# Mixture-of-experts phase: GpSimd's gathers and scatters written out with indices taken from the table, expert numbers read once per tile, 71 blocks in place of 72

## The reference, cut to what matters

```python
logits = jnp.einsum('th,eh->te', x, gate_w)            # 8 experts
probs = jax.nn.softmax(logits.astype(jnp.float32), axis=-1)
topk_w, topk_i = jax.lax.top_k(probs, K)               # K = 2
...
g = jnp.einsum('th,ehi->eti', x, w_gate)               # 256 -> 352
u = jnp.einsum('th,ehi->eti', x, w_up)
eo = jnp.einsum('eti,eih->eth', jax.nn.silu(g) * u, w_down)
out = jnp.einsum('te,eth->th', combine, eo)
so = jax.nn.silu(x @ sw_gate) * (x @ sw_up) @ sw_down  # the shared expert
out = out + sg * so
```

## Time and profile before

| | us |
|---|---|
| median of 3 runs (2241.15 to 2248.3) | 2243.68 |
| the profiled execution, device time | 2245.09 |
| its span in the trace | 2243.4 |
| TensorE busy | 2090.2 (93%) |
| VectorE busy | 1318.9 (59%) |
| ScalarE busy | 1020.1 (45%) |
| GpSimd busy | 449.9 (20%) |

### The profile page before, as it was taken

How to read it: one execution, slowest core, us unless ns; L and a number is a source line. 1 busy time by engine, 2 the same in 40 slices (tenths; PEclk the granted TensorE clock), 3 DMA queues, 4 the chain that set the end, 5 groups by cost and what they waited for, 6 DMA issues and landing times. The chain is left out here.

```text
span 2243.4 us, 51733 instructions
## 1 busy us (share of the span) xinstructions
PE 2090.2 (93%) x18596; PEld 1403.1 (63%) x18597; DVE 1318.9 (59%) x2444; ACT 1020.1 (45%) x2049; POOL 449.9 (20%) x643
## 2 busy tenths in 40 slices
PE   6899799999999958999999999999988999999997
PEld 6577676766666734345556555555548676666665
DVE  5455448222222866789999999999725662222237
ACT  2211122222222123378989898898974222222221
POOL 1022100444444044400000000000000014444420
PEclk9999769999999979999999999999997899999999
DMA  7000010111111329601111111110032001111125
GB/s 282 0 1 0 22 54 3 54 56 56 57 58 54 122 70 218 160 22 45 46 49 40 47 46 46 43 45 20 3 151 93 11 19 57 56 57 58 58 80 178
DMA packets 92766, 142.37 MB, mean 63 GB/s; under 512 B 28724, under 2 KB 65844, under 8 KB 91380
## 3 DMA queue, kind: packets, MB, share of 16 engines
q1 hardware_dynamic: 77620, 98.02, 14.5%
q0 software_dynamic: 14976, 41.96, 5.7%
HBM read 91.04 MB, written 48.50 MB: 62 GB/s over the span
## 5 line engine op out<-in xcount | busy, mean ns | idle before, releaser
L1663 ACT ACTIVATE att_scores_pt<-att_scores_psE 128x512 f32<-128x512 f32 x1024 | 598.4, 598 | 68.4 <-PE att_scores_psE L1273 26.6
L1288 DVE TENSOR_REDUCE att_mx<-att_scores_psS 128x1 f32<-128x1024 f32 x472 | 578.1, 1225 | 50.0 <-PE att_scores_psS L1273 18.9
L592 PE MATMUL moe_ps<-W_gate_up,work 128*128 (+1 forms) x1664 | 535.3, 465 | 2.4 <-ACT work L269 1.2
L1273 PE MATMUL att_scores_psE<-att_qs,att_ks 99*32 99x512 bf16 x4096 | 436.7, 382 | 5.1 <-DVE att_scores_psO L1693 4.3
L592 PEld LDWEIGHTS moe_ps<-W_gate_up,work 128*128 128x128 f32 x1664 | 302.2, 192 | 143.5 <-issue 10.0
L615 PE MATMUL moe_ps<-W_down,moe_hidT 128*128 (+1 forms) x1248 | 318.6, 391 | 15.5 <-DVE moe_hidT L459 4.2
L1765 PE MATMUL att_scores_psO<-att_scores_pt,att_va 128*17 128x256 f32 x4096 | 330.0, 379 | 2.9 <-ACT att_scores_osb L1668 1.3
L1273 PE MATMUL att_scores_psS<-att_ks,att_qs 96*32 96x512 bf16 x3776 | 308.1, 380 | 0.1
L454 DVE TENSOR_TENSOR moe_hid<-moe_silu,moe_ps 128x352 f32<-128x352 f32 x208 | 108.3, 521 | 312.0 <-PE moe_ps L592 312.0
L615 PEld LDWEIGHTS moe_ps<-W_down,moe_hidT 128*128 128x128 f32 x1248 | 221.5, 190 | 65.3 <-issue 36.0
L273 ACT ACTIVATE moe_silu<-moe_ps 128x352 f32<-128x352 f32 x208 | 96.6, 464 | 337.9 <-PE moe_ps L592 337.9
(11 more groups left out here) (266 smaller groups left out, 2030.2 us busy)
## 6 DMA issues: line engine op xcount, KB each, us to landing
work<-expert_rows SPq DMA_DIRECT2D x64, 256.0 KB, 2.8
W_gate_up<-in_gate_up_dram SPq DMA_DIRECT2D x2, 6336.0 KB, 22.0
query_key_parts<-att_qkv_parts SPq DMA_DIRECT2D x32, 384.0 KB, 3.9
att_qs<-query_key_parts SPq DMA_DIRECT2D x96, 128.0 KB, 2.7
att_ks<-query_key_parts SPq DMA_DIRECT2D x96, 128.0 KB, 2.6
normalised_rows<-work SPq DMA_DIRECT2D x64, 128.0 KB, 1.7
W_down<-in_down_a_dram SPq DMA_DIRECT2D x2, 2304.0 KB, 27.0
values<-att_qkv_vt SPq DMA_DIRECT2D x32, 136.0 KB, 4.0
```

What stands on the lines that cost most here:

```text
L592: last = nc.tensor.matmul(bank[u][:, 0:I], srcT[u][:, k, :], W["gate_up"][:, k, e, half * I:(half + 1) * I], start=(k == 0), stop=(k == KD ...
L1273: last = nc.tensor.matmul(out[j:j + 32, :], stationary[:, j:j + 32], moving, start=True, stop=True, tile_position=(0, j), skip_group_check ...
L1288: return nc.vector.tensor_reduce(a.mx[g % 2][:, v:v + 1], bank[:, :, :].rearrange("p h k -> p (h k)"), AX.X, ALU.max)
L1663: nc.scalar.activation(pt[s % 2][:, r, :], psE[use % E_BANKS][:, :], ACT.Exp, scale=HD ** -0.5).then_inc(p_ready, 1)
```

## The change

- GpSimd: `fetch` no longer copies indices and no longer drains. Gather and scatter take their indices from `slots_i[:, j, 0:1]` and `slots_i[:, j, 1:2]`. Since j must be a plain number for that, the loop is gone and all blocks are written out.
- TensorE: `step` hands the expert's number on in a register. `next_e` is read behind `rows_in` of the tile ahead, and `before_e` is the register of the tile just done. At a loop's first tile nothing is handed on.
- `NB` is 71; the table keeps its 72 columns (`NBT`). The counts that buffers 0 to 5 wait for at the end are now `sent_by(u)`: 12 blocks for buffers 0 to 4 and 11 for buffer 5. VectorE peels 7 tiles in place of 6. TensorE's loop has the same 11 rounds, with two routed tiles behind it in place of three.

```diff
-            def fetch(j, u, free=None):
-
-                if free is not None:
-                    pool.wait_ge(y_sent[u], free)
+            def fetch(j):
+
+                u = j % SRC
+                if j >= SRC:
+                    pool.wait_ge(y_sent[u], j // SRC * 16)
                     pool.sem_inc(due, 1)
-                nc.gpsimd.tensor_copy(now_i[u][:, :], slots_i[:, j, :])
-                pool.drain()
                 nc.gpsimd.indirect_dma_start(
                     out=src[u][:, :], out_offset=None, in_=xn_d,
-                    in_offset=bass.IndirectOffsetOnAxis(ap=now_i[u][:, 0:1].bitcast(U32), axis=0)
+                    in_offset=bass.IndirectOffsetOnAxis(ap=slots_i[:, j, 0:1].bitcast(U32), axis=0)
                 ).then_inc(src_loaded[u], 16)
...
-            with pool.Fori(1, NB // SRC - 1) as jj:
-                for u in range(SRC):
-                    fetch(jj * SRC + (u + AHEAD), (u + AHEAD) % SRC, jj * 16 + (16 if u + AHEAD >= SRC else 0))
-                    send(jj * SRC + u, u)
-            for j in range(NB - SRC, NB):
+                fetch(j)
+            for j in range(NB):
                 if j + AHEAD < NB:
-                    fetch(j + AHEAD, (j + AHEAD) % SRC, (j + AHEAD) // SRC * 16)
-                send(j, j % SRC)
+                    fetch(j + AHEAD)
+                send(j)
...
+                here_e, before_e = known if known is not None else (expert(n, k), None)
                 if here:
                     hidden_T(n - 1, (here - 1) % 2)
-                gate_up(n, here % 2, expert(n, k))
+                gate_up(n, here % 2, here_e)
...
+                next_e = expert(n + 1, kind(here + 1)) if more else None
+                if here and before_e is None:
+                    before_e = expert(n - 1, kind(here - 1))
                 if here:
-                    down(n - 1, (here - 1) % 2, expert(n - 1, kind(here - 1)), kind(here - 2) if here >= 2 else None)
+                    down(n - 1, (here - 1) % 2, before_e, kind(here - 2) if here >= 2 else None)
+                return next_e, here_e
```

More of the change, by code:

```diff
@@ L21 @@
 KI = IP // P
-NB = (TOKENS * TOPK) // P + E
-SLOTS_ALL = NB * P
+NBT = (TOKENS * TOPK) // P + E
+NB = NBT - 1
+SLOTS_ALL = NBT * P
 ROWS_ALL = TOPK * TOKENS
@@ L102, in ffn_phase @@
         posf = sb("posf", [P, CH])
-        iota_p = sb("iota_p", [P, P], BF16); iota_j = sb("iota_j", [P, NB], BF16)
+        iota_p = sb("iota_p", [P, P], BF16); iota_j = sb("iota_j", [P, NBT], BF16)
         tile1 = sb("tile1", [P, CH], BF16)
         lane = sb("lane", [P, 1])
-        dump = sb("dump", [P, NB])
+        dump = sb("dump", [P, NBT])
         hot_p = [sb(f"hot_p{u}", [P, PIECE, P], BF16) for u in range(2)]
[L108 to L115, removed]
+        hot_j = sb("hot_j", [P, PIECE, NBT], BF16)
+        hot_id = [sb(f"hot_id{u}", [P, PIECE, 2, NBT], BF16) for u in range(2)]
+        place = sb("place", [P, NBT]); empty = sb("empty", [P, NBT])
+        slots_i = sb("slots_i", [P, NBT, 2], I32)
+        ble = sb("ble", [1, NBT, E])
+        bex = sb("bex", [1, NBT])
+        bexi = sb("bexi", [1, NBT], I32)
         ps = [ctx.enter_context(nc.psum_tensor(f"{tag}_ps{i}", [P, 512], F32)) for i in range(8)]
@@ L159, in ffn_phase @@
         buffer = lambda n0, u, k: (n0 - NA + u) % SRC if k == "routed" else (n0 + u) % 2
+        sent_by = lambda u: 16 * len(range(u, NB, SRC))
+        ROUNDS = NB // SRC
+        PEELED = 6 + NB % 2
         FOUND = 4 + CH // PIECE + 1
@@ L176, in _ @@
             for u in range(SRC):
-                sp.wait_ge(y_sent[u], 16 * (NB // SRC))
+                sp.wait_ge(y_sent[u], sent_by(u))
             for t in range(GS):
@@ L190, in _ @@
                            allow_small_or_imprecise_dtypes=True)
-            nc.gpsimd.iota(iotab[:, :], [[1, NB]], base=0, channel_multiplier=0,
+            nc.gpsimd.iota(iotab[:, :], [[1, NBT]], base=0, channel_multiplier=0,
                            allow_small_or_imprecise_dtypes=True)
@@ L221, in send @@
                 nc.gpsimd.indirect_dma_start(
-                    out=ys, out_offset=bass.IndirectOffsetOnAxis(ap=now_i[u][:, 1:2].bitcast(U32), axis=0),
-                    in_=yb[u % 2][:, :], in_offset=None).then_inc(y_sent[u], 16)
+                    out=ys, out_offset=bass.IndirectOffsetOnAxis(ap=slots_i[:, j, 1:2].bitcast(U32), axis=0),
+                    in_=yb[j % 2][:, :], in_offset=None).then_inc(y_sent[j % SRC], 16)
             pool.wait_ge(slots_ready, 1)
@@ L468, in source @@
                 if sent:
-                    dve.wait_ge(y_sent[u], 16 * (NB // SRC))
+                    dve.wait_ge(y_sent[u], sent_by(u))
                 else:
@@ L512, in _ @@
                 step(n, n, 0, "shared", finding.get(n, (lambda: one_hots(n - 4)) if 0 <= n - 4 < CH // PIECE else None))
-            with dve.Fori(0, (NB - 6) // 2) as i:
+            with dve.Fori(0, (NB - PEELED) // 2) as i:
                 for u in range(2):
                     step(i * 2 + (NA + u), NA, u, "routed")
-            for n in range(LAST - 6, LAST):
+            for n in range(LAST - PEELED, LAST):
                 step(n, n, 0, "routed")
@@ L649, in _ @@
                     with pe.Fori(0, times) as i:
+                        known = None
                         for u in range(UNROLL[k]):
-                            step(i * UNROLL[k] + (n0 + u), n0, u, k, i)
-                else:
-                    step(n0, n0, 0, k)
+                            known = step(i * UNROLL[k] + (n0 + u), n0, u, k, i, known, u + 1 < UNROLL[k])
+                    known = None
+                else:
+                    known = step(n0, n0, 0, k, 0, known, n0 + 1 < NS and n0 + 1 not in looped and n0 + 1 != NA)
+                    known = known if known[0] is not None else None
             hidden_T(NS - 1, (NS - 1) % 2)
```

30 lines of the change are left out of this document (14 added, 16 removed).

## The result

The changed kernel takes 2186.06 us (median of 4 runs, 2183.86 to 2187.8); the kernel before, run beside it, takes 2245.39. The ratio is 0.9733, with a 95% interval of 0.9718 to 0.9748: 2.7% faster. The profiled executions are 2245.09 us before and 2185.97 after, 59.1 us apart. The forecast was 46.2 us less on the same footing and 2198 us in all, with a range of 2188 to 2210.

The account below looks back on a forecast made before the run. GpSimd's 4.58 us round was taken to bound the routed tiles; 45.6 us from the routed stretches and 0.6 from the entries made 46.2 us saved, giving 2198 us, range 2188 to 2210.

Parts of the forecast that it names:

- What bounds the kernel: Routed tiles: GpSimd's round of drain, copy, issue and gather sets the pace, 4.58 us a block.
- Copy and drain gone, gap 0.30 us: GpSimd's routed blocks: gather follows scatter by 0.30 us instead of 2.10, making the round 2.58 us.
- Rival A: GpSimd: the 2.10 us gap belongs to the gather, so its round is 4.38 us and the kernel 2203; chance 0.12.
- B: GpSimd: a fresh index column costs 2.10 us, so scatters pay too, 6.18 us a block, about 2455 us; chance 0.03.
- The expert number handed on, 4.29 to 4.21 us: TensorE's routed tile: one read fewer ahead of gate and up shortens it from 4.29 to 4.21 us.
- The round's edge: TensorE's loop round of six tiles: 0.31 us as today plus 0.20 for a third read, 25.77 us in all.
- Rival D: TensorE's loop: the round's extra 0.51 us vanishes, 11 us over 22 rounds, kernel 2187 us; no separate chance given.
- C: TensorE keeps its 4.29 us tile with GpSimd out of the way: 10.6 us less gained, 2209 us; chance 0.10.
- Blocks 0 to 2 as now: Start of each routed stretch, `y_out` of block 0 to block 2: stays at 8.76 us.
- Entry: First routed tile's wait for its gather: 0.3 us saved per phase, 0.6 in all, bounds 0 and 1.
- 71 blocks: Routed stretches: one tile, gather and scatter fewer per phase; the two tiles gone are some 8.5 us.
- The first late tile's source: Buffer 1 waits for a scatter only two tiles back: just fits, else below 1 us once per phase.

Follow-up runs that it names:

- e3: Changed kernel with GpSimd's index copy and drain put back before each gather, TensorE still reading each expert number once: 2233.8 us.
- e5: Changed kernel with a drain ahead of each gather and no index copy: 2233.7 us.
- e1: Changed kernel with TensorE reading the expert's number twice per tile again, once between hidden transposes and gate and up: 2200.6 us.
- e6: Changed kernel with two expert reads per tile on TensorE, both ahead of the down product: 2185.5 us.
- e8: Changed kernel with all 72 blocks in place of 71: 2192.6 us.
- e9: Changed kernel with a drain ahead of each scatter and none ahead of gathers: 2273.6 us.
- e4: Changed kernel with GpSimd's index copy put back, ordered to the gather by a semaphore in place of the drain: 2187.5 us.
- e10: Kernel before the change (loop, 72 blocks, two reads) with one edit, a semaphore from index copy to gather in place of the drain: 2212.2 us.
- e2: Changed kernel with TensorE's two reads and GpSimd's index copy and drain put back, leaving the written-out stream and 71 blocks: 2231.4 us.
- e7: Changed kernel with VectorE's table of slots made one tile earlier and the blocks' experts one tile later: 2181.2 us.

## Why the prediction was right and where it was wrong

- **What bounds the kernel**: right. GpSimd's round of 4.58 us did, and with the drain back it does again (e3, e5).
- **Copy and drain gone, gap 0.30 us**: right in size and in the drain as its cause. What I did not see is what the drain waits for. The chain's 1.60 us on the drain and 1.89 of "issue" looked like a price of the drain plus one of the gather. The drain's own record runs from 1990.38 to 1993.54 us; the scatter, started at 1990.99, landed at 1993.43. So the drain lies over both pieces, and only the 0.7 us from its end to the gather at 1994.28 are the gather's start. Rival A (the gap stays with the gather) and B (a fresh index costs it) fell with the changed kernel itself: its gathers take a fresh index from the table, at a gap of 0.30 us, and its scatters, with a fresh index too, start 0.81 to 0.85 us behind `y_out`, like the 0.81 before.
- **The expert number handed on, 4.29 to 4.21 us**: right in size. The reason, the read's place behind the hidden transposes, was right too; e1 and e6 show it.
- **The round's edge, the term that failed.** I wrote "The third read adds between nothing ... and about 0.46 us ...; I take 0.20. A round is then 6 x 4.21 + 0.31 + 0.20 = 25.77 us." It measured 25.28, so the 0.51 us of edge is 0: 11 rounds by 0.49 us by 2 phases are 10.8 of the 12.9 us that I missed. I carried the 0.31 us over from the kernel before as if it were a fixed price of the round. Part of it was no edge at all (with 4.31 us tiles, as e1 has them, some 0.1 us of it is in the tiles); the rest was the price of an edge met without a lead, and the edit that I had costed at 0.08 us per tile also restored the lead (0.12 to 0.87 us, e1). The third read I put at 0.20 us, though all reads of that tile lie under gate and up. Rival D had this time, 2187, and I gave it no chance of its own and no mechanism; I even wrote that forecast, A and C span 2187 to 2210, and then cut the range at 2188, 2 us above the median.
- **Blocks 0 to 2 as now, 8.76 us**: measured 8.51 (413.22 - 404.71), 0.5 us over both phases.
- **Entry, 0.6 us for both phases**: mis-sized, it was 4.0. From one gate and up to the next, over the wait for the first gather, it went from 395.00 - 386.71 = 8.29 to 396.42 - 390.67 = 5.75 us in the first phase, and from 6.83 to 5.41 in the second. The first gather starts 0.31 and 0.28 us behind the table that it needs, where it was 1.20 and 1.10: 0.8 to 0.9 us a phase in place of my 0.3. In the first phase there is the clock besides. From 386 to 403 us its mean granted share was 0.90 before and 1.00 after: before, it stood at the lower of its two levels, 1.2 GHz, for 3.4 us from 391.5 us on, right behind the idle 2.18 us; after, it stayed at the higher one, 2.4 GHz, behind an idle 1.31. The idle 2.40 us of the second phase before did not bring it down, so what made it fall in the first stays open. The down product's six matmuls took 2.77 us before and 1.46 after. The kernel before, then the changed one:

```profile
386.71 2.53 PE L592 MATMUL moe_ps<-W_gate_up,work 128*128 128x352 f32 x8
...
391.90 2.77 PE L615 MATMUL moe_ps<-W_down,moe_hidT 128*128 128x256 f32 x6
...
395.00 2.53 PE L592 MATMUL moe_ps<-W_gate_up,work 128*128 x8
```

```profile
394.79 1.46 PE L611 MATMUL moe_ps<-W_down,moe_hidT 128*128 128x256 f32 x6
...
396.42 2.53 PE L588 MATMUL moe_ps<-W_gate_up,work 128*128 x8
```

  I had taken for this gather the 0.81 us that a scatter needs behind its wait, and had left the clock out.
- **71 blocks**: 4.21 us per phase for an empty tile, as taken (e8). **The first late tile's source** on buffer 1: no stall.
- **What the sum adds up to.** The stretches gave 57.2 us where I had 45.6, so 11.6 of the 12.9 us are theirs, and the entries gave 3.4 us more than I had. Against these gains the memory layer of the profiled execution was longer after than before: the first routing tile of the first phase starts at 275.84 us in place of 271.90, a loss of 3.9 us that is not the change's. The rest, a gain of some 2 us, lies in stages that no edit touches. Without the memory layer's loss the forecast would have missed by more, so it was luck that the time came as near to the range as it did.

## What to carry to other kernels

A drain on the engine that issues indirect transfers is a wait for the landing of the transfer in flight, so order an index copy by its own semaphore, or take indices from where they lie; that one edit did 34 of the 59 us. Put a register read where the longest products lie ahead of it on the engine, and not right ahead of the next group of matmuls. When an edit gives an instruction stream its lead back, re-cost every small stall that was measured without one (a register read, a loop's edge): here they went together.

## What the runs showed of the hardware

- GpSimd's drain ends 0.07 to 0.12 us behind the landing of the transfer in flight. The next transfer starts 0.7 to 0.8 us after the drain's end (e5, e9).
- TensorE's sequencer starts the register work of gate and up 0.87 us ahead of the matmul in the changed kernel and in e6 (0.7 to 0.8 us in a round's first tile), and 0.10 to 0.12 us with a register read of 0.3 us between two short groups of matmuls (e1); the tile is 0.08 to 0.12 us longer then.
- Once per phase, always at block 54, the changed kernel's scatter starts 3.34 us behind the end of its `y_out` instead of 0.85, and so it does in every kernel of the study in which GpSimd does not drain, e4 (with the copy), e8 (72 blocks) and e10 (with the loop) among them. GpSimd's timeline there:

```profile
630.49 0.97 POOL L215 DMA_INDIRECT work<-normalised_rows,moe_slots_i  x1 [0.30 <-issue]
635.90 1.00 POOL L224 DMA_INDIRECT expert_rows<-work,moe_slots_i  x1 [4.44 <-issue]
```

  It cost nothing here: the round in which it falls takes 25.27 us as the others do. Its cause stays open.
- The memory layer, which no kernel of the study changes, ends up to 7.5 us apart from one to the next: the first routing tile starts at 268.30 us in e2, 270.95 in e7 and 275.84 in the changed kernel. In the changed kernel the mean granted share of the clock from 50 to 200 us is 0.94, in e7 0.97: it stands at the lower level, 1.2 GHz, for 17 and for 10 of these 150 us, and else at 2.4 GHz. Busy times in that stretch, with the clock as the third number from the end, of the changed kernel and of e7:

```profile
50.00:200.00 150.00, 133.60 (x637) 105.85 (x638) 78.05 (x382) 33.98 (x88) 21.57 (x21) 0.94 0.00 1
```

```profile
50.00:200.00 150.00, 133.00 (x653) 105.58 (x652) 78.52 (x386) 34.63 (x91) 21.57 (x21) 0.97 0.00 1
```

  Why the clock falls in one and not in the other stays open. In the changed kernel's run beside e7 that tile starts at 274.31, so 3.4 of e7's 5.6 us lie there and should not be counted as the edit's.
